# Second attention on one Trainium2 core: where TensorE does a slot's projection

## The reference

```python
q = decoder_output @ wq_w + wq_b
k = encoder_output @ wk_w + wk_b
v = encoder_output @ wv_w + wv_b
...
score = jnp.einsum('bhqd,bhkd->bhqk', q, k) / jnp.sqrt(jnp.asarray(KEY_SIZE, dtype=jnp.float32))
score = score * mask
score = jnp.where(score == 0, jnp.float32(NEG_INF), score)
alignment = jax.nn.softmax(score, axis=-1)
context = jnp.einsum('bhqk,bhkd->bhqd', alignment, v)
context = context.transpose(0, 2, 1, 3).reshape(b, -1, H * KEY_SIZE)
heads = context @ wo_w + wo_b
```

## Time and profile before

| | |
|---|---|
| median of 3 runs | 1925.39 us (1922.57 to 1934.13) |
| the profiled execution | 1911.46 us, of which the span of the trace is 1909.8 us |
| PE busy over the span | 1471.8 us (77%) |
| DVE busy | 1291.2 us (68%) |
| ACT busy | 1111.0 us (58%) |
| mean granted TensorE clock | 0.896 of full speed |

### The profile page before, as it was taken

The page is one execution under the profiler, slowest core; times in us unless marked ns, Lnnn a source line. Parts: engine busy times, 40 slices in busy tenths (PEclk is TensorE's granted clock), DMA queues, the critical chain, the costliest instruction groups (busy, mean ns, idle before and its releaser), DMA issues. The chain is left out here.

```text
span 1909.8 us, 42846 instructions
## 1 busy us (share of the span) xinstructions
PE 1471.8 (77%) x15716; PEld 1052.9 (55%) x15717; DVE 1291.2 (68%) x3175; ACT 1111.0 (58%) x2236; POOL 222.1 (12%) x223
## 2 busy tenths in 40 slices
PE   1899999999999729007488988988836888888880
PEld 1566766766666525007265666666524666666660
DVE  6567677777767684775488988888877753444443
ACT  5466666666666434654388888888823753333330
POOL 4300010010000040200500000000003400000006
PEclk9999999999999969558599999999956888999995
DMA  4100010010000000000100000000006631111104
GB/s 137 49 18 18 18 34 18 18 31 21 18 18 10 30 21 0 0 0 18 39 13 25 25 25 14 25 25 17 2 12 225 217 120 37 33 33 33 33 23 118
DMA packets 50258, 74.99 MB, mean 39 GB/s; under 512 B 5625, under 2 KB 37202, under 8 KB 50098
## 3 DMA queue, kind: packets, MB, share of 16 engines
q1 hardware_dynamic: 45346, 60.86, 10.5%
q0 software_dynamic: 4752, 11.93, 1.9%
HBM read 51.95 MB, written 20.82 MB: 38 GB/s over the span
## 5 line engine op out<-in xcount | busy, mean ns | idle before, releaser
L517 ACT ACTIVATE a_pt<-a_ps_t 125x336 f16<-125x336 f32 x256 | 102.7, 448 | 107.6 <-PE a_ps_t L448 107.3
L1170 ACT ACTIVATE a_p<-a_s,a_nb 112x375 f32<-112x375 f32 x256 | 140.8, 598 | 28.3 <-DVE a_nb L1271 28.2
L289 PE MATMUL a_ps_o<-a_vh,a_pt 125*128 125x64 f16 (+1 forms) x1536 | 152.9, 183 | 3.4 <-ACT a_pt L1183 0.8
L291 PE MATMUL a_ps_o<-a_vh,a_pt 125*128 125x64 f16 (+1 forms) x1536 | 151.2, 182 | 0.0
L290 PE MATMUL a_ps_o<-a_vl,a_pt 125*128 125x64 f16 (+1 forms) x1536 | 151.0, 182 | 0.0
L1095 PE MATMUL a_ps_t<-ident,a_p 112*128 112x112 f32 x768 | 117.7, 283 | 41.7 <-ACT a_p L1170 40.8
L509 ACT ACTIVATE a_p<-a_ps_s,a_nb 112x375 f32<-112x375 f32 x256 | 143.8, 573 | 3.7 <-DVE a_scaled L589 3.7
L289 PEld LDWEIGHTS a_ps_o<-a_vh,a_pt 125*128 125x128 f16 x1536 | 133.3, 98 | 17.1 <-ACT a_pt L1183 8.7
L290 PEld LDWEIGHTS a_ps_o<-a_vl,a_pt 125*128 125x128 f16 x1536 | 130.8, 98 | 10.9
L1271 DVE CUSTOM_DVE_ANT_0 a_s<-a_s,a_fill 112x375 f32<-112x375 f32 x256 | 129.9, 546 | 5.5
L289 PE MATMUL e_p<-e_xth,wh 128*128 128x128 f16 x560 | 128.3, 229 | 6.8 <-issue 6.6
(11 more groups left out here) (330 smaller groups left out, 4669.2 us busy)
## 6 DMA issues: line engine op xcount, KB each, us to landing
w_stage<-in_w SPq DMA_DIRECT2D x72, 256.0 KB, 3.2
a_ctx<-in_ctxT SPq DMA_DIRECT2D x16, 375.0 KB, 3.6
ctx<-a_cx SPq DMA_DIRECT2D x16, 375.0 KB, 4.5
a_cx<-ctx SPq DMA_DIRECT2D x16, 375.0 KB, 3.2
slots_in<-r_zeros SPq DMA_DIRECT2D x1, 4480.0 KB, 15.8
e_xt<-slots_in SPq DMA_DIRECT2D x35, 128.0 KB, 2.0
slots_out<-e_y POOLq DMA_DIRECT2D x35, 128.0 KB, 2.0
a_mask<-in_mask SPq DMA_DIRECT2D x16, 164.1 KB, 2.4
```

The lines of the kernel that those rows point to most:

```text
L289: nc.tensor.matmul(out, wh, mh, start=(i == 0), stop=False)
L291: last = nc.tensor.matmul(out, wl, mh, start=False, stop=(i == n - 1))
L517: nc.scalar.activation(pt[:, g % 2, i, 0, :, 0:S], ps_t[0:KV, i, 0:NKV * S].rearrange("p (t s) -> p t s", t=NKV), ACT.Copy).then_inc(pt_hi, 1)
L1170: nc.scalar.activation(p32[:, g % 2, i, 0:NC], s2[:, g % 2, i, :], ACT.Exp, bias=nb[:, g % 2, i:i + 1], scale=-1.0).then_inc(exp_done, 1)
```

## The change

Inside the slot loop of TensorE, the projection is issued ahead of the transposes; before, it came behind them. Nothing else is touched: the same instructions, the same waits on each of them, and the lists of the other four engines are the same.

```diff
             for g in range(SLOTS):
                 if g < G:
                     scores(g)
+                for name, b in slot_job(g):
+                    job(name, b)
                 if 0 <= g - 1 < G:
                     transposes(g - 1)
-                for name, b in slot_job(g):
-                    job(name, b)
                 if 0 <= g - 2 < G:
                     weighted_values(g - 2)
                 if 0 <= g - 1 < G:
                     take_high(g - 1)
```

## The result

The changed kernel took 2040.41 us (median of 6 runs, 2027.68 to 2044.4) against 1931.35 us (median of 6) for the kernel before: a ratio of 1.0559, with a 95% interval of 1.0519 to 1.0599. It is 109 us slower; the forecast was 64 us slower, at 1989, and the range ended at 2012. The profiled execution took 2035.14 us, with a span of 2033.5. Of all the runs in this document one execution, of `v0_back` (2027.68 us), was in a slower state than the others of its kernel and is left out of its ratio.

What follows compares the result with a forecast made beforehand. The prediction saw no engine far ahead in the second attention, the loop between TensorE, ScalarE and VectorE setting the pace. It added 52 us for longer slots and 12 for the clock to 1925.39: 1989 us, range 1966 to 2012.

Steps and rivals of the forecast that it cites:

- the clock term: Second attention, TensorE's granted clock: pauses come oftener, twice the 11 falls at 1.06 us each, 12 us more.
- The place and the sign: Second attention: projections wait for VectorE and hold back the transposes and the chain behind them; slower, 64 us in all.
- the last part of the prediction: Signs in the profile: transposes' wait for exponentials nearly gone, projections waiting for VectorE instead, 1.6 to 1.7 us behind Q.
- The sum for a batch at full clock: Eight slots of the second attention: 29.9 us against 26.44, 3.46 more, times 15 batches 52 us.
- V0's start: V0's projection in its slot: held by VectorE's low part of Q, it starts 2.21 us into the slot.
- the tail of a slot: From first transpose to next scores: a chain of 2.07 us, read from the slot without a job.
- the price of 1.06 us for every fall: Cost of one fall from 2.4 to 1.2 GHz: a batch of 27.50 us against 26.44 at full clock.
- The rival of the clock: Second attention: the clock falls much more, three falls a batch, 39 us on top of 52, 2016 us; chance 0.12.
- The lower end of my range, 1966: Whole kernel's predicted range, 1966 to 2012; its fast side was 1977 with no more falls, less 8 for scatter, 1969.
- My chance of 0.91 for slower by over 1%: Whole kernel: slower by over 19 us, from the forecast and the clock's rival together, 0.91.
- The pauses that I named for this rival: V0's slot: two pauses over half a us next to one of 1.7; OT's slot: one of 0.8.
- a mean clock in the phase under 0.88: Second attention: sign that would make the prediction wrong; 22 falls would leave the mean clock at about 0.93.

Runs made afterwards that it cites:

- v0_back: The changed kernel, but in V0's slot the transposes stand ahead of the projection again; 1.0287 of the kernel before.
- after_fill: The changed kernel plus unread matmuls: 12 in V0's slot, 6 in OT's, 4 per projection slot ahead of the weighted values; 1955.68 us, 1.0116 of the kernel before.
- fill_wait: The changed kernel plus unread matmuls only where a projection waits for VectorE, 12 in V0's slot and 6 in OT's; 1.0240 of the kernel before.

## Why the prediction was wrong

The change cost 109 us where 64 were forecast. The step that failed is the clock term.

**The place and the sign were right.** The projections wait for VectorE, hold back the transposes, and behind them the chain to take_high; no other engine's list moved. The transposes' wait for the exponentials went, as the last part of the prediction said; longer ones took its place, ScalarE's for the transposes above all (166.6 us where it had been 10.3).

**The sum for a batch at full clock was right within 0.7 us.** 29.9 was forecast, 29.22 measured with the clock held: 42 us instead of 52. V0's start was forecast at 2.21 and came at 2.22, K1's at 0.70 and came at 0.73, OT's at 1.31 and came at 1.43. What was too large was the tail of a slot. I took 2.07 + 0.08 us from the first transpose (or the end of the job) to the next scores. Behind a job it is 1.96 in K1's slot (1091.64 - 1089.68), with no 0.08 ahead of it: where a job stands ahead, both heads' exponentials are long done, and the two groups of transposes follow each other closer than in the slot that I read the piece from (0.74 us instead of 0.85). ScalarE's L1179 starts 1090.46 - 1089.68 = 0.78 behind them, not 0.89. Against that the K0 job starts at 0.58 of its slot, not 0.50.

**The term that failed is the clock.** "I take twice the falls: 11 x 1.06 = 12 us" measured 61. The price of a us at the lower level was about right: a batch has 0.10 x 27.32 = 2.7 us of it before, for 0.87 us, and 0.40 x 34.13 = 13.7 us after, for 4.91 us, so 0.32 and 0.36 us for each. The count of the falls was not far off either: 11 were worked out and 11 are there before; 22 were forecast and 29 came, which at 1.06 us each would be 19 us more and not 61. What failed is the price of 1.06 us for every fall. It is that of the falls before, which last 3.4 us; in the changed kernel half of them lasted 10.2 us, and the time at the lower level rose fivefold. Nothing in the rows that I had read showed a fall in this phase that lasts longer.

Why they last longer stays open. I think that a fall lengthens TensorE's work in the next slots, delays the splits and so makes the next pause, which would feed itself; the pattern below fits that, but no run shows it apart. The runs show what goes along with it: the long stretches vanish when the pauses are filled (`after_fill`), and all but one do when V0 alone goes back (`v0_back`).

**The rival of the clock was the right one, and too cheap.** I gave it 0.12 and a ceiling of three falls a batch at 1.06 us, 39 us; 61 came, from only two falls a batch. (The lower end of my range, 1966, should have been the 1969 that its own parts give; this changes nothing.) My chance of 0.91 for slower by over 1% was borne out. The pauses that I named for this rival, V0's and OT's, have a part in it, but are not the whole: with both filled the clock is 0.96, and with only the short ones filled it is 0.96 too.

The section of the Trainium skill that the prediction named ("TensorE: Matmul & The Clock Gate", "A second HAM failure mode: psum-queue depth-cycling") says that frequent short pauses make the clock swing and cost throughput. The trace agrees in direction: the mean granted clock is 0.80 with pauses in every slot with a projection, and 1.00 with the same order and filled pauses. But in `fill_wait`, where only the short pauses are left, it is 0.96, so that short pauses alone don't account for the loss here.

**A sign that the prediction named came:** "a mean clock in the phase under 0.88" was to make it wrong. It was 0.80.

## What to carry to other kernels

On an engine that works in order, ask two things before moving a piece of work ahead of a wait: whether that piece is itself ready, and whether it ran under another engine's work where it stood. Here V0 was not ready for 1.6 us, and K1 and V1, which had run under ScalarE's copy, cost 0.6 us each in front of the chain, their short waits included. Where the granted clock of a stage already dips, as here at 0.95, price a change that adds pauses at both levels of the clock and not with a proportional share of falls: one fall may last longer than another, here 10.2 us beside 3.4. Work added in the pauses tells in one run how much of a loss is the clock's. In this kernel such added matmuls, and the empty slot behind the slowest split, took 0.8% off the kernel before.

## What the runs showed of the hardware

The loop and the clock locked into one pattern: from slot 8 on, each of 14 batches of the changed kernel took 34.09 to 34.17 us, with the same two stretches at 1.2 GHz, 10.2 us from the middle of OT's slot and 3.4 us from V0's projection, 34.1 us apart from batch to batch. Just as unexpected, 12 matmuls of 240 columns ahead of V0 and 6 ahead of OT, some 2 us of work a batch that nobody reads (one starts every 0.10 us), took away as much of the loss (4.1 of 4.9 us a batch) as 28 spread over seven slots.
